# Adding the value bias to V during the projections instead of to the attention output

## The reference

```
Q, K, V = h @ Wq.T + bq, h @ Wk.T + bk, h @ Wv.T + bv      # h = layernorm(x)
Q, K = rope(Q), rope(K)
x = x + softmax(causal(Q K^T / sqrt(32))) @ V @ Wo.T + bo
h = layernorm(x)
x = x + (silu(h @ gate.T * gs) * (h @ up.T * us)) @ down.T * ds
```

## Time and profile before

| | |
|---|---|
| median of 3 runs | 752.11 us (748.64 to 752.68) |
| the profiled execution | 749.88 us |
| its span in the trace | 748.2 us |
| PE busy | 732.0 us, 98% |
| DVE, ACT, POOL busy | 443.8, 310.9, 247.7 us |
| granted clock of PE | 0.999 of full speed |

### The profile page before, as it was taken

The page is one execution under the profiler, slowest core; times in us unless marked ns, Lnnn a source line. Parts: engine busy times, 40 slices in busy tenths (PEclk is TensorE's granted clock), DMA queues, the critical chain, the costliest instruction groups (busy, mean ns, idle before and its releaser), DMA issues.

```text
span 748.2 us, 10633 instructions
## 1 busy us (share of the span) xinstructions
PE 732.0 (98%) x3563; PEld 539.3 (72%) x3563; DVE 443.8 (59%) x1071; ACT 310.9 (42%) x641; POOL 247.7 (33%) x224
## 2 busy tenths in 40 slices
PE   8999999999999999999999999999999999999996
PEld 7887888766656666666666548788788888888885
DVE  6978684897778787777878545853243125114113
ACT  3322231266666666666666662222332232222221
POOL 0816152411114242333324245822232223223223
PEclk9999999999999999999999999999999999999999
DMA  8686469635576667676667356540001001001001
GB/s 280 230 284 232 162 254 309 255 115 160 162 192 172 185 172 194 168 188 164 187 162 187 102 185 225 222 201 1 0 20 38 0 1 56 0 0 56 1 1 59
DMA packets 54318, 104.39 MB, mean 140 GB/s; under 512 B 14820, under 2 KB 18404, under 8 KB 53748
## 3 DMA queue, kind: packets, MB, share of 16 engines
q1 hardware_dynamic: 54264, 103.72, 44.0%
HBM read 69.62 MB, written 38.21 MB: 144 GB/s over the span
## 4 chain that ended last, share of the span: by engine, by line
PE 81%; DVE 6%; issue 5%; DMA 3%; POOL 2%; ACT 1%; SPq 1%; DVEq 0%; POOLq 0%; ACTq 0%
PE ps L1105 32%; PE ps L1244 18%; PE ps L1130 10%; PE ps L1223 10%; PE ps L1320 9%; DMA x_st<-in_x 1%; PE ps L1097 1%; POOL hid_lo L592 1%; DVE xn L786 1%; DVE stats L771 1%; DMA rec_l<-rec_rows 1%; DMA w_st<-in_wk 1%; DMA l_cols<-o_raw 1%; ACT p L683 0%; DVE esin L893 0%
## 5 line engine op out<-in xcount | busy, mean ns | idle before, releaser
L683 ACT ACTIVATE p<-ps 128x384 f32<-128x384 f32 (+3 forms) x384 | 162.0, 489 | 58.0 <-PE ps L1223 57.8
L843 DVE CUSTOM_DVE_ANT_0 masked<-ps,mask_qk 128x512 bf16<-128x512 f32 (+1 forms) x240 | 113.2, 500 | 56.6 <-PE ps L1130 55.7
L1244 PE MATMUL ps<-p,v_slot 128*64 128x512 f32 (+3 forms) x768 | 137.3, 494 | 0.2 <-ACT o_raw L690 0.2
L1223 PE MATMUL ps<-q_st,k_st 99*128 99x384 f32 (+2 forms) x384 | 135.7, 361 | 1.1 <-ACT p L683 1.0
L1056 DVE SCALAR_TENSOR_TENSOR hid<-ps,us_sb,silu 128x512 f32<-128x512 f32 x44 | 33.0, 751 | 165.2 <-PE ps L1105 159.5
L1130 PE MATMUL ps<-k_st,q_st 96*128 96x512 f32 (+2 forms) x384 | 128.9, 357 | 2.0 <-DVE row_max L843 1.7
L592 POOL TENSOR_TENSOR hid_lo<-hid,hid_hi 128x512 fp32r<-128x512 f32 x44 | 56.8, 1290 | 173.0 <-ACT hid_hi L758 173.0
L561 POOL TENSOR_SCALAR_AFFINE_SELECT p<-p 128x512 f32<-128x512 f32 x64 | 40.6, 635 | 209.0 <-ACT p L683 209.0
L1244 PEld LDWEIGHTS ps<-p,v_slot 128*64 128x64 f32 x768 | 50.1, 136 | 74.2 <-issue 62.2
L1130 PEld LDWEIGHTS ps<-k_st,q_st 96*128 96x128 f32 x384 | 72.3, 189 | 29.7 <-DVE row_max L843 14.3
L1223 PEld LDWEIGHTS ps<-q_st,k_st 99*128 99x128 f32 x384 | 72.1, 189 | 16.9 <-issue 6.3
(11 more groups left out here) (117 smaller groups left out, 1080.8 us busy)
## 6 DMA issues: line engine op xcount, KB each, us to landing
qk_scratch<-st_hi SPq DMA_DIRECT2D x32, 512.0 KB, 3.6
q_st<-qk_scratch SPq DMA_DIRECT2D x32, 384.0 KB, 3.8
k_st<-qk_scratch SPq DMA_DIRECT2D x32, 384.0 KB, 4.8
flag_st<-in_ffn SPq DMA_DIRECT2D x32, 264.0 KB, 2.8
ffn_copy<-in_ffn SPq DMA_DIRECT2D x32, 264.0 KB, 3.5
qk_scratch<-st_lo SPq DMA_DIRECT2D x16, 512.0 KB, 3.7
o_T<-o_raw SPq DMA_DIRECT2D x32, 128.0 KB, 4.2
rec_l<-rec_rows SPq DMA_DIRECT2D x32, 128.0 KB, 3.3
```

The costliest lines, as they stand in the source:

```text
L683: act.activation(p32[:, at:at + q0 + w - keep], ps[:, ST_BANK + i % ST_RING, keep - q0:w], ACT.Exp, scale=SCALE).then_inc(exp_done, 1)
L843: ins = dve.tensor_tensor_reduce((masked_a if u < 2 else masked)[:, s_before(i) % 2, col:col + kept], scores, mask_qk[:, 512 - kept:512], ...
L1223: pe.matmul(ps[:, ST_BANK + i % ST_RING, 0:w], k_st[0:K_ALL, slot, kt * P:(kt + 1) * P], q_st[0:K_ALL, slot, q0:q0 + w], start=True, stop= ...
L1244: ins = pe.matmul(ps[VW * a:VW * (a + 1), o_bank(u, half), q0 - 512 * half:512], v_slot[:, slot, kt, :], p32[:, at:at + n], start=(kt == 0 ...
```

## The change

bv is added to V itself. POOL gets sixteen adds of 128x512 (one for each token tile of V): twelve stand behind the rotations of chunks 1 to 3, one behind each, and four behind `mask_p` of steps 0 to 3. The eight adds of bv to a group of `o_T` (128x1024) go. For the new form bv is loaded spread over all partitions (256 KB) instead of as 128x4 values. It takes the place of Wo in `load_late()`, since the two share memory with the weight staging; Wo (1 MB) is loaded in step 4 of stage B, after all biases are added. `bo`, `ds` and the first half of `xr` are loaded inside step 31, and the second half of `xr` last of all. POOL adds `bo` to the first `xr` half before it scales group 6, not after it.

```diff
             def load_late():
                 sp.wait_ge(w_lo_done, 4)
                 sp.wait_ge(v_lo_done, 2)
-                sp.dma_start(wo_st[:, :, :], wo).then_inc(wo_in, 16)
+                sp.dma_start(bv_sb[:, :], bv.partition_broadcast(P)).then_inc(bv_in, 16)
...
                 sp.dma_start(ffn_copy[:, cols], ffn[:, cols]).then_inc(ffn_copied, 16)
+                if t == HEADS - 1:
+                    sp.wait_ge(pv_half[1], PAIRS - 1)
+                    sp.dma_start(bo_sb[:, :], bo.partition_broadcast(P)).then_inc(c_in, 16)
+                    sp.dma_start(ds_sb[:, :], ds.partition_broadcast(P)).then_inc(c_in, 16)
+                    sp.wait_ge(v_copied, HEADS)
+                    load_x(xr[:, 0, :, :], 0).then_inc(xr_in[0], 16)
                 if t % 4 == 3 and t >= 7:
                     load_rec((t - 7) // 4)
+                if t == SLOTS:
+                    sp.wait_ge(v_biased, N_CH * TJ)
+                    sp.dma_start(wo_st[:, :, :], wo).then_inc(wo_in, 16)
...
-            sp.wait_ge(v_copied, HEADS)
-            load_x(xr[:, 0, :, :], 0).then_inc(xr_in[0], 16)
-            load_x(xr[:, 1, :, :], 1).then_inc(xr_in[1], 16)
             move_pair(PAIRS - 2)
             sp.wait_ge(pv_half[1], PAIRS)
-            sp.dma_start(bo_sb[:, :], bo.partition_broadcast(P)).then_inc(c_in, 16)
-            sp.dma_start(ds_sb[:, :], ds.partition_broadcast(P)).then_inc(c_in, 16)
             move_pair(PAIRS - 1)
             store_rec(GROUPS - 1)
             load_rec(GROUPS - 1)
+            load_x(xr[:, 1, :, :], 1).then_inc(xr_in[1], 16)
...
+            def add_value_bias(n):
+
+                b, kt = divmod(n, KT)
+                if n == 0:
+                    pool.wait_ge(bv_in, 16)
+                pool.wait_ge(v_ready, n + 1)
+                pool.tensor_tensor(v_sb[:, b, kt, :], v_sb[:, b, kt, :], bv_sb[:, :], ALU.add).then_inc(v_biased, 1)
...
                     if n < 2:
                         value_weight_lo(4 + n)
+                    if c > 0:
+                        add_value_bias(TJ * (c - 1) + p)
...
                 b, h = divmod(t, NH)
-                pool.wait_ge(v_ready, TJ * CC * (b + 1))
+                pool.wait_ge(v_biased, TJ * CC * (b + 1))
...
                 pool.tensor_tensor(o_T[:, g, :], o_T[:, g, :], rec_l[:, :], ALU.mult).then_inc(o_scaled, 1)
-                pool.wait_ge(o_scaled, g + 1)
-                pool.tensor_scalar(o_T[:, g, :], o_T[:, g, :], bv_sb[:, g % KC:g % KC + 1], None, ALU.add).then_inc(o_done, 1)
...
                 mask_p(t)
-
-
-            scale_group(GROUPS - 2)
+                if t < TJ:
+                    add_value_bias(TJ * (N_CH - 1) + t)
...
             pool.wait_ge(c_in, 32)
             add_bias(0)
+            scale_group(GROUPS - 2)
             scale_group(GROUPS - 1)
             add_bias(1)
```

More of the change, by code:

```diff
@@ L133, in transformer_block @@
         bqk_sb = sb("bqk_sb", [P, 8], F32)
-        bv_sb = sb("bv_sb", [P, KC], F32)
+        sb("bv_place", [P, KC], F32)
         gs_sb = sb("gs_sb", [P, IT], F32)
@@ L159, in transformer_block @@
             xst_c = sb("xst_c", [P, TJ, H], F32, after_wo)
+        with ExitStack() as before_wo:
+            bv_sb = sb("bv_sb", [P, H], F32, before_wo)
         wo_st = sb("wo_st", [P, KC, H], F32)
@@ L255, in transformer_block @@
         v_ready = sem("v_ready")
+        bv_in = sem("bv_in")
+        v_biased = sem("v_biased")
         slot_ones = sem("slot_ones")
@@ L280, in transformer_block @@
         o_scaled = sem("o_scaled")
-        o_done = sem("o_done")
         wo_in = sem("wo_in")
@@ L372, in _ @@
                     sp.dma_start(sin_sb[:, :], sin).then_inc(const_in, 16)
-                    with nc.allow_non_contiguous_dma(reason="one bias for each partition"):
-                        sp.dma_start(bv_sb[:, :], bv.rearrange("(k p) -> p k", p=P)).then_inc(const_in, 16)
                     sp.dma_start(gs_sb[:, :], gs).then_inc(const_in, 16)
@@ L515, in _ @@
                                pattern=[[-1, 512]], channel_multiplier=1).then_inc(consts, 1)
-            pool.wait_ge(const_in, 96)
+            pool.wait_ge(const_in, 80)
             def value_weight_lo(n):
@@ L629, in _ @@
             weight_hi(3)
-            act.wait_ge(const_in, 96)
+            act.wait_ge(const_in, 80)
             for c in range(N_CH):
@@ L731, in _ @@
             output_weight_hi(1)
-            act.wait_ge(o_done, KC)
+            act.wait_ge(o_scaled, KC)
             for j in range(TJ):
@@ L737, in _ @@
                 if c == 1:
-                    act.wait_ge(o_done, 2 * KC)
+                    act.wait_ge(o_scaled, 2 * KC)
                 for j in range(TJ):
@@ L881, in _ @@
             weight_lo(2)
-            dve.wait_ge(const_in, 96)
+            dve.wait_ge(const_in, 80)
             for c in range(N_CH):
```

## The result

The changed kernel took 753.72 us (median of 20 runs, 750.20 to 757.18), the kernel before 749.66 in 20 runs of its own (748.00 to 755.81). The ratio is 1.0033, 95% interval 1.0016 to 1.0049. The interval leaves out 1. The size is about 2.5 us by the ratio and 4.1 us by the two medians, so at or near the half per cent (3.8 us) that the prediction called "the same". The median lies inside its range, but the change is on the other side of its forecast of −0.3 us.

The account below looks back on a forecast made before the run. PE was taken as the bound, busy 732.0 of 748.2 us, so only its stalls could give. Span: 748.2 − 1.2 + 1.0 − 0.1 = 747.9, 0.3 less; median 751.8 us, range 747.4 to 754.5.

Parts of the forecast that it names:

- a gain of 1.2 us: Output projection, 470 us: without the add of bv, PE's whole 1.2 us wait for `oT_lo` goes.
- by the low end nothing is lost: Output projection: `xr` half 1 lands at 464.5 to 469.0; the early end costs nothing, the late end some 0.8 us.
- The price of one add that meets the `xn`: Chunks 1 and 2: a POOL add beside DVE's four `xn` costs DVE 1.0 us, bounds 0 and 1.29.
- The stall at 62 us: Chunk 1 of the projections: PE's wait for `ocos` grows from 0.6 to 1.6 us.
- the term that I took at −0.1 with a bound of −1.0: Chunk 1 loads: with Wo's load gone from there, `x_st` lands earlier; taken at −0.1 us, bounds 0 and −1.0.
- Rival (c): Attention stage, near 203 us: Wo's load holds up the row maxima, +4.6 us, time 756.4; chance 0.05.
- costs of the adds in steps 0 to 3: Attention stage: the four adds there lie beside PE's full stretch and cost zero.
- The eight adds removed there: Attention stage: taking these adds off POOL can't be seen beside PE's full stretch, zero.
- its cover of 1.3 us: Chunk 2: `ocos` ends 1.3 us before PE wants it, covering a price of 1.0; without it 1.0 more.
- Rival (b): Projections or output projection: port lock costs more, +1.4, or second `xr` half late, +1.8; about 753.7 us; chance 0.17.

Follow-up runs that it names:

- run 1: Changed kernel with the small strided load of bv put back at the start, its data unused; 752.18 us, ratio 1.0010.
- run 5: The changed kernel again, without an edit, as control on one chip; 753.70 us, ratio 1.0018.
- run 3: Changed kernel with `xr` half 1 issued right behind half 0, in step 31; 752.54 us, ratio 1.0012.
- run 6: Changed kernel with the old order of loads and group 6 scaling at the end of the attention stage, adds kept; 750.72 us, ratio 0.9992.
- run 7: Kernel before with only the new order at the end of the attention stage, bv still added to the outputs; 753.47 us, ratio 1.0012.
- run 4: Changed kernel without the sixteen adds of bv, so that bv is left out of the result; 751.25 us, ratio 1.0007.
- Run 10: Changed kernel with `xr` half 1 loaded behind the 2.8 MB of gate weights instead of ahead of them; 758.49 us, ratio 1.0112.
- run 12: The kernel before again, without an edit, profiled once more; 750.58 us, ratio 1.0004.
- run 2: Kernel before with the small load of bv moved from the start to behind the load of Wo; 751.86 us, ratio 1.0007.
- run 8: Changed kernel with `xr` half 1 issued right behind half 0 and the adds of bv to V one rotation later; 751.59 us, ratio 0.9988.
- run 9: Changed kernel with the old order at the end of the attention stage and the adds of bv one rotation later; 750.34 us, ratio 0.9996.
- run 11: Changed kernel with the old order at the end of the attention stage and each add of bv done three times; 762.44 us, ratio 1.0143.

## Why the prediction was wrong

**The step that failed** is the last half sentence of the first part: "a gain of 1.2 us, all of the stall and no more, because behind it PE is the limit again", with "by the low end nothing is lost" for the loads. Both halves failed.

- *Behind it PE is not the limit.* The prediction followed the moved loads to the end of the output projection and stopped. It priced half 1 as late or not late for `residual`, but never the load queued behind it. Half 1 went out next to `wg_sb` and the third `xr` load, and the third landed 15.0 us after its issue instead of 10.6. That gave PE's waits for `xst_c` and `xT_lo`, 1.1 us, a step of 1.5; runs 1 and 5 have the same waits (1.5 and 1.3), and run 3, with half 1 sent out early, has none. In time, run 6 against run 5 gives 1.3 ± 0.6 for the order, and run 7 against before 1.5 ± 0.35, though there at another place; run 4 gives nothing, so the size is open. Run 10 shows what a late half 1 becomes with one more load ahead: 3.2 more.
- *The gain wasn't there on average.* The stall for `oT_lo` was in the first of the two profiles of the kernel before and not in the second (run 12), nor in run 2, whose tail is the same. In the profile of the changed kernel it is gone, and the trace shows 1.2 us fewer there, yet a mean over runs can only gain the part of it that a typical execution has.

**The start** gave most of the difference of the two profiles, 3.8 of 6.0 us, and was not in the prediction. The low clock in PE's first products, and V of chunk 0 late by 3.0 to 3.8 us, are in the profiles of the changed kernel and runs 1, 5 and 6, and not in runs 3, 4, 8 to 11, which have the same start, nor in the four profiles with the kernel before at their base. Late first weights are in the first of them alone. In runs 1, 5 and 6 PE had waited 1.9 to 2.0 us for `xn`, but so it had in run 2, whose start is fast. Run 1 has the low clock with the removed load back in place. Four of ten against none of four is no proof of a link; what decides it stays open. The mean of span times one minus the clock is 3.7 to 4.1 us in the changed kernel's runs and 3.1 to 4.1 in those of before (with the part behind PE's last product in both), so at most about 1 us of the difference goes by this.

**What held:**
- The price of one add that meets the `xn`: predicted 1.0, measured 0.97, and runs 8, 9 and 12 at 3.88 without it. Of the rule of the Trainium skill that the prediction weighed (page "SBUF — State Buffer", section "Who interferes with whom"), by which the whole instruction of 1.29 us would be lost: the trace gives 0.97, so the measurement decides against the full length.
- The stall at 62 us was predicted at 1.6 and was 0.55, because `x_st` landed 1.0 us sooner, the term that I took at −0.1 with a bound of −1.0. The profile of the changed kernel sits at the bound. That Wo's leaving did it isn't shown: with Wo at its old place DVE waited 4.4, 2.5, 3.0 and 3.7 us for `x_st` (before, 12, 2, 7), with Wo moved 2.7 to 3.9, and no run moves Wo alone. And the kernel before had no stall there in runs 2 and 12, so from a typical execution the adds cost PE something. From chunk 1's first Q and K to its V, six profiles with adds that meet the `xn` (the changed kernel, runs 1, 3, 5, 6, 10) take between 0.24 us less and 0.23 us more than the first profile of before; six in which nothing new meets them (2, 4, 7, 8, 9, 12) take 0.67 to 0.85 us less. That is some 0.8 us for the adds, nearly the 1.0 of the forecast, but with nothing to cancel it. In time, adds alone cost 0.2 ± 0.4 (run 6 against before), and moving them out of the way gave 0.7 ± 0.5 (run 6 to 9).
- Wo inside stage B cost nothing: it landed in 8.7 us and PE stood nowhere near 203 us. Rival (c) is refuted, as are costs of the adds in steps 0 to 3. The eight adds removed there gave nothing back, as said.
- Chunk 2 stayed inside its cover of 1.3 us: no wait for `ocos` there in the profile of the changed kernel.
- Rival (b) had half the right mechanism: it let half 1 be late for the output projection, and the runs have the load behind it late. Its number, 753.7, is the measured median, but in part by luck: it was reckoned from 752.11, the median of three runs of the kernel before, where twenty gave 749.66.

So of some 1.5 to 2 us by span times clock (748.30 and 747.79 against 746.3 to 746.6), runs 5 to 7 and the profiles give the order of the tail about 1.4 and the meeting with the `xn` some 0.8 at most. Runs 1 and 4, on another chip, don't bear this sum out: the changed kernel with the small load back lost only 0.6 ± 0.4, and without the adds nothing was left to lose. The two causes are seen in the traces; how the lost time divides between them stays open.

## What to carry to other kernels

When a load is moved next to other loads, price the loads queued behind it as well as its own consumer: follow each until it has landed and its reader has been served. A stall of 1 us that hangs on a landing is no gain until a second profile of the same kernel has it too; a second profile of the kernel before (run 12) has neither of the two in this sum. And an add on GpSimd costs what it slows on VectorE just then: beside the `xn` 1 us of VectorE, one place later in the program's order nothing measurable.

## What I had not expected of the hardware

- One kind of 1 MB load (`xr`) took 5.6 us with nothing large issued just ahead of it, 10.6 with 2.8 MB issued 2.7 us ahead, and 15.0 with 1 and 2.8 MB issued in the 2 us ahead. Between the two profiles of the kernel before, the waits for `rec_l` and `x_st` differ by 1.7 and 1.9 us, more than any term of the sum.
- In four of the fourteen profiles PE's level fell 10.0 to 11.6 us into the span, and eight matmuls took 1.9 to 2.1 us instead of 1.1 to 1.2. With DVE's `w_lo` falling beside POOL's behind it, V of chunk 0 came 3.0 to 3.8 us late. In all four PE had waited 1.3 to 2.0 us for `xn` just before, but in run 2 it had waited 1.95 and kept the full clock.
- DVE's `xn` lost 0.97 us for the first POOL add beside them, and 0.98 more with two more adds (4.85 to 5.83). Taking 1.94 us as their time alone, 3.88, 4.85 and 5.83 are two, three and four POOL instructions of 0.97 us each; the last add of three cost the `xn` nothing.
